# Experts' attention: the value product in quarters set between the two scores of a step, and four small products one step later

## What is computed

```python
def expert_step(acc, params):
    qw, qb_, kw, kb_, vw, vb_, ow, ob_, g = params
    q = (x @ qw.T + qb_).reshape(B, S, H, Dh).transpose(0, 2, 1, 3)
    ...
    scores = jnp.einsum('bhqd,bhkd->bhqk', q, k) * scale
    p = jax.nn.softmax(scores, axis=-1)
    o = jnp.einsum('bhqk,bhkd->bhqd', p, v)
    o = o.transpose(0, 2, 1, 3).reshape(B, S, E) @ ow.T + ob_
    return (acc + o * g[..., None], None)
```

## Time and profile before

| | |
|---|---|
| time, median of 3 runs | 2183.87 us (2181.33 to 2192.77) |
| profiled execution: its time, its span | 2187.13 us, 2185.3 us |
| mean granted TensorE clock | 0.942 |
| PE, DVE, ACT, POOL busy over the span | 85%, 77%, 59%, 43% |
| stage b, first and last record of the mix | 199.9 and 1098.8 us |

### The profile page before, as it was taken

The page is one execution under the profiler, slowest core; times in us unless marked ns, Lnnn a source line. Parts: engine busy times, 40 slices in busy tenths (PEclk is TensorE's granted clock), DMA queues, the critical chain, the costliest instruction groups (busy, mean ns, idle before and its releaser), DMA issues. The chain is left out here.

```text
span 2185.3 us, 50731 instructions
## 1 busy us (share of the span) xinstructions
PE 1855.6 (85%) x20464; PEld 954.8 (44%) x20464; DVE 1673.8 (77%) x2850; ACT 1288.2 (59%) x1848; POOL 941.1 (43%) x914
## 2 busy tenths in 40 slices
PE   5758999999999999999947898988888988988984
PEld 3542233233233333333223665665665655665663
DVE  3856777777777777777647978889878889879873
ACT  4423666666666666666725656666655656656652
POOL 0011111111111111111029958768768768768760
PEclk8956999999999999999968999999999999999998
DMA  1032223222323232323014333333333333333320
GB/s 36 1 76 50 49 57 58 50 55 55 64 60 65 60 64 60 64 60 61 2 39 119 89 95 103 100 96 107 95 96 103 100 95 103 100 96 102 95 69 15
DMA packets 101281, 156.36 MB, mean 72 GB/s; under 512 B 29335, under 2 KB 64185, under 8 KB 97209
## 3 DMA queue, kind: packets, MB, share of 16 engines
q1 hardware_dynamic: 98937, 152.19, 28.5%
q10 hardware_dynamic: 2112, 0.94, 0.3%
HBM read 98.03 MB, written 51.12 MB: 68 GB/s over the span
## 5 line engine op out<-in xcount | busy, mean ns | idle before, releaser
L824 DVE TENSOR_REDUCE ENM<-PM 128x1 f32<-128x512 f32 x1024 | 665.4, 687 | 212.3 <-PE PM L604 199.9
L735 ACT ACTIVATE EPT<-PA 128x1024 f32<-128x1024 f32 x512 | 514.6, 1021 | 214.7 <-PE PV L627 124.2
L604 PE MATMUL PM<-EKX,EQX 48*128 48x512 bf16 x1024 | 381.3, 393 | 18.9 <-DVE ENM L824 17.9
L1300 POOL TENSOR_TENSOR DRN<-DRN,DHALF 128x8 f32<-128x8 f32 x192 | 371.7, 1936 | 0.0
L524 POOL CAST ENMP<-ENM 128x16 bf16<-128x16 f32 x64 | 12.7, 198 | 748.0 <-DVE ENM L824 748.0
L627 PE MATMUL PV<-EPT,EVP 128*32 128x256 f32 x4096 | 327.9, 392 | 2.1 <-ACT EAVS L766 1.9
L1298 POOL TENSOR_TENSOR DQR<-DR 128x512 f32<-128x512 f32 x192 | 252.5, 1315 | 169.0 <-DVE DR L1581 169.0
L616 PE MATMUL PA<-EQX,EKX 51*128 51x512 bf16 x1024 | 254.6, 387 | 19.4 <-DMA EQX<-EROWS 15.4
L1344 PE MATMUL PM<-DWQKV,DXS 128*128 128x512 f32 x384 | 214.4, 641 | 26.9 <-ACT DRAW L1500 20.3
L604 PEld LDWEIGHTS PM<-EKX,EQX 48*128 48x128 bf16 x1024 | 93.8, 93 | 308.9 <-DVE ENM L824 222.0
L1500 ACT ACTIVATE DRAW<-PM 128x512 f32<-128x512 f32 x192 | 114.6, 597 | 169.5 <-DVE DR L1581 93.1
(11 more groups left out here) (207 smaller groups left out, 2858.2 us busy)
## 6 DMA issues: line engine op xcount, KB each, us to landing
DV<-d_vpark SPq DMA_DIRECT2D x192, 256.0 KB, 4.9
d_vpark<-DVT SPq DMA_DIRECT2D x48, 512.0 KB, 2.6
e_park<-EPARTS SPq DMA_DIRECT2D x64, 192.0 KB, 3.0
EQX<-e_park SPq DMA_DIRECT2D x32, 384.0 KB, 5.6
EKX<-e_park SPq DMA_DIRECT2D x32, 384.0 KB, 9.2
DWQKV<-in_WqkvR SPq DMA_DIRECT2D x6, 1536.0 KB, 10.0
e_park<-EPARTS SPq DMA_DIRECT2D x64, 128.0 KB, 2.7
e_park<-EPARTS SPq DMA_DIRECT2D x64, 64.0 KB, 2.1
```

Source lines behind the costliest of these rows:

```text
L604: pe.matmul(PM[:, r, :], lhsT=QX[64 * r:64 * r + KQ, b, hp, t * 128:(t + 1) * 128], rhs=KX[64 * r:64 * r + KQ, b, hp, :], start=True, stop ...
L735: s_.activation(PT[:, kt, pair * 2 * S:(pair + 1) * 2 * S], PA[:, 2 * pair:2 * pair + 2, :].rearrange("p a b -> p (a b)"), ACT.Exp, scale= ...
L824: v.tensor_reduce(NM[:, g % 2, t, j, 0:1], PM[:, r, :], AX.X, ALU.max, negate=True).then_inc(maxed, 1)
L1300: g.tensor_tensor(rn, rn, HALF[:, 0:8], ALU.pow).then_inc(rooted.sem, 1)
```

## The change

`mix` takes quarters of 128 queries in place of halves of 256; the count that its semaphore reaches doubles, and the waits of the exponential and of `mix_out` are rewritten to the same points. `key_major` takes the heads r that it is to do. In a step TensorE now does: `key_major` of head 0, a quarter, `key_major` of head 1, `query_major` r = 0, a quarter, `query_major` r = 1. In step 3 the two quarters stand behind everything, as the half did. The products for "v" and "ont" go from step 5 to 6 and "o" from 6 to 7, on TensorE, ACT and DVE.

```diff
     if g % HG == 1 and more:
-        u += [(5, "v")]
+        u += [(6, "v")]
     if g % HG == 0 and not (first and g == 0):
-        u += [(5, "ont"), (6, "o")]
+        u += [(6, "ont"), (7, "o")]
...
-                    for r in range(2):
+                    for r in rs:
                         mm = pe.matmul(PA[:, 2 * pair + r, :], lhsT=KX[64 * r:64 * r + KS, b, hp, kt * 128:(kt + 1) * 128],
                                        rhs=QX[64 * r:64 * r + KS, b, hp, :], start=True, stop=True)
-                    mm.then_inc(kscored, 1)
-
-                def mix(e, g, kt, half):
-
-                    k, c = e * NG + g, S // 2
+                    if 1 in rs:
+                        mm.then_inc(kscored, 1)
+
+                def mix(e, g, kt, part):
+                    k, c = e * NG + g, S // 4
...
                     for s in range(8):
-                        key_major(e, g, s)
+                        key_major(e, g, s, (0,))
+                        if s != 3:
+                            mixes(s, 0)
+                        key_major(e, g, s, (1,))
                         scores_ahead(s, (0,))
                         if s != 3:
-                            mixes(s)
+                            mixes(s, 1)
                         scores_ahead(s, (1,))
                         if s == 3:
-                            mixes(s)
+                            mixes(s, 0)
+                            mixes(s, 1)
...
-                        act.wait_ge(mixed, 8 * k + (2 * kt - 6))
+                        act.wait_ge(mixed, 16 * k + (4 * kt - 12))
...
-                    act.wait_ge(mixed, 8 * k + 8)
+                    act.wait_ge(mixed, 16 * k + 16)
...
-                        if s == 6 and "o" in uses:
+                        if s == 7 and "o" in uses:
                             add_out(gp // HG, use(e, g, "o"))
```

More of the change, by code:

```diff
@@ L605, in query_major, with key_major @@
                                   rhs=KX[64 * r:64 * r + KQ, b, hp, :], start=True, stop=True).then_inc(qscored, 1)
-                def key_major(e, g, s):
+                def key_major(e, g, s, rs):
                     f = (e * NG + g) * 8 + s
@@ L610, in key_major @@
                     hp = 2 * (g % HG) + pair
-                    if s == 0:
+                    if s == 0 and 0 in rs:
                         pe.wait_ge(rows_in, (e * NG + g) * 64 + 64)
-                    if not (isinstance(f, int) and f < 2):
+                    if 0 in rs and not (isinstance(f, int) and f < 2):
                         pe.wait_ge(exped, f - 1)
-                    for r in range(2):
+                    for r in rs:
                         mm = pe.matmul(PA[:, 2 * pair + r, :], lhsT=KX[64 * r:64 * r + KS, b, hp, kt * 128:(kt + 1) * 128],
                                        rhs=QX[64 * r:64 * r + KS, b, hp, :], start=True, stop=True)
-                    mm.then_inc(kscored, 1)
-                def mix(e, g, kt, half):
-                    k, c = e * NG + g, S // 2
+                    if 1 in rs:
+                        mm.then_inc(kscored, 1)
+                def mix(e, g, kt, part):
+                    k, c = e * NG + g, S // 4
                     pe.wait_ge(exped, k * 8 + (2 * kt + 2))
-                    if kt == 0 and half == 0 and not (isinstance(k, int) and k == 0):
+                    if kt == 0 and part == 0 and not (isinstance(k, int) and k == 0):
                         pe.wait_ge(mixed_out, k)
                     for j in range(4):
-                        mm = pe.matmul(PV[32 * j:32 * j + 32, half * c:half * c + c], lhsT=VP[:, g // HG, kt, 4 * (g % HG) + j, :],
-                                       rhs=PT[:, kt, j * S + half * c:j * S + half * c + c],
-                                       start=kt == 0 and half == 0, stop=kt == TB - 1, skip_group_check=True)
+                        mm = pe.matmul(PV[32 * j:32 * j + 32, part * c:part * c + c], lhsT=VP[:, g // HG, kt, 4 * (g % HG) + j, :],
+                                       rhs=PT[:, kt, j * S + part * c:j * S + part * c + c],
+                                       start=kt == 0 and part == 0, stop=kt == TB - 1, skip_group_check=True)
                     mm.then_inc(mixed, 1)
@@ L641, in scores_ahead, with mixes @@
                             query_major(e2, g2, s + LEAD - 16, rs)
-                    def mixes(s):
+                    def mixes(s, i):
                         kt, half = divmod(s - 3, 2)
                         if kt >= 0:
-                            mix(e, g, kt, half)
+                            mix(e, g, kt, 2 * half + i)
                         elif not (first and g == 0):
-                            mix(ep, gp, kt + TB, half)
+                            mix(ep, gp, kt + TB, 2 * half + i)
                     for s in range(8):
-                        key_major(e, g, s)
+                        key_major(e, g, s, (0,))
+                        if s != 3:
+                            mixes(s, 0)
+                        key_major(e, g, s, (1,))
                         scores_ahead(s, (0,))
                         if s != 3:
-                            mixes(s)
+                            mixes(s, 1)
                         scores_ahead(s, (1,))
                         if s == 3:
-                            mixes(s)
+                            mixes(s, 0)
+                            mixes(s, 1)
                         for step, what in slot_uses(first, last, g):
@@ L718, in _ @@
                     slot(NE - 1, g, False, True)
-                for kt, half in ((TB - 2, 1), (TB - 1, 0), (TB - 1, 1)):
-                    mix(NE - 1, NG - 1, kt, half)
+                for kt, part in ((TB - 2, 2), (TB - 2, 3)) + tuple((TB - 1, i) for i in range(4)):
+                    mix(NE - 1, NG - 1, kt, part)
                 pe.wait_ge(mixed_out, NE * NG)
```

## The result

The changed kernel takes 2296.2 us (median of 4, 2262.5 to 2338.1) against 2182.7 for the kernel before on the same chips; the ratio is 1.043 (95% interval 1.037 to 1.050). The forecast was 2206, in a range of 2186 to 2235: the direction was right, the size was not. The mean granted TensorE clock goes with the time: 0.883 (2338 us), 0.902 (2298), 0.903 (2295), 0.921 (2262), where the kernel before has 0.942.

A forecast was written before the change was run, and what follows sets the result against it. Stage b was taken as paced by TensorE in some steps, DVE or ACT in others, with TensorE pacing every step without another wait afterwards. Plain slots +20 and pairs +2 gave +22 us, 2206 on the median; range 2186 to 2235.

The forecast's parts named there:

- The price of a quarter: Stage b, TensorE: a quarter is 0.34 to 0.36 us long, taken as 0.36, with 0.32 on the way in.
- the step of 1.36: Stage b: a step at TensorE's own pace goes from 1.10 to 1.36 us, above DVE's 1.20.
- the late exponential: Plain slot: step 4's exponential on ACT starts at R + 1.63 instead of 1.13, delaying step 7 by 0.50 us.
- the sum of +22 at full clock: Whole kernel: +20 us from 32 plain slots and +2 us from 16 pairs of groups 0 and 1.
- the +0.64 of a plain slot: Groups 2, 3, 6, 7: from R (start of "rows") to the next R, 13.06 us instead of 12.42.
- The pair ends where it did, 0.07 later: Groups 0 and 1: where the wait for the rows' DMAs stands, the pair's end moves only 0.07 us.
- The waits for EON: Groups 0 and 1: moving "ont" and "v" takes away two waits of 0.98 us.
- DVE's wait for PM: Stage b: DVE's wait for scores in PM goes up from 185 us by some 20.
- Absorbed: Rival, plain slot: step 7 stays at 5.23, the slot costs +0.14, +6 us in all, 2190; chance 0.14.
- faster: Rival, stage b: a quarter with way in costs 0.445, half of a half; 18 us faster, 2166; chance 0.12.
- the loads bind: Rival, stage b: a quarter takes the half's 0.57, step 1.78, about 2390 us; chance 0.04.
- dearer meetings: Rival, stage b: each new meeting of kinds costs 0.05 to 0.1 more, 2235 to 2265 us; chance 0.08.

The follow-up runs named there:

- the pair of filled kernels: Unread products ahead of the rows' wait in group 2, added to the changed kernel (2238.7 us) and to the kernel before (2213.6 us).
- quarters_between_keys: Changed kernel with both quarters of a step together between the two `key_major`: 2239.4 us, ratio 1.026.
- quarters_dense_behind: Changed kernel with five unread 128 x 512 float32 products behind step 0 of group 2: 2270.7 us, ratio 1.043.

## Why the prediction was wrong

- **The step that failed** is one sentence of the sum: "Clock: stage b is at 1.00 and the gaps shrink, so no change." I read 1.00 as a property of a busy engine, and so put the clock into the sum at nothing. It was one of the old order, which had the full clock back 3.4 us after each of its two falls. The new order does not: in the profiled execution 300 us of stage b ran at 1.2 GHz, where a step is 2.26 instead of 1.36 us. By 1 - 1.36 / 2.26 = 0.40 of 300 that is about 120 of the 147 us by which stage b grew; 25 are the dearer order, as the pair of filled kernels shows. That is the longest of the four runs; the median grew by 114 us, with less low clock.
- The gaps did not vanish either: the rows' wait stood at 0.8 to 2.4 us in group 2 of all later experts (4.5 in the first). A wait of 1.57 us was enough once, and was not another time.
- The price of a quarter, the step of 1.36, the late exponential and the sum of +22 at full clock held: 0.36, 1.36, R + 1.63 and 25.1 us. But the +0.64 of a plain slot (0.68 measured) came right with a wrong share in it. I had put 0.50 on the late exponential and taken the dearer steps 4 to 6 as hidden behind it. Measured, these steps alone bring step 7 to R + 5.50, and the exponential adds 0.12.
- Groups 0 and 1: 17.11 for group 0, and 14.39 for a group 5, which has the jobs of group 1 and mostly no wait; forecast 17.14 and 14.26. "The pair ends where it did, 0.07 later" does not hold: in the second to the seventh expert, all at full clock there, groups 0 and 1 took 0.4 to 1.6 us longer with their wait. Groups 4 and 5 took 0.8 less to 0.1 more where they ran at full clock, so little of this shows in the sum. That the wait hangs on SP's loads was an assumption too: swapping them gained no time. What ends that wait stays open.
- The waits for EON are gone, as forecast. DVE's wait for PM went to 319 us, not to 205: that is the low clock again.
- Of the rivals none had the clock in it. "Absorbed", "faster", "the loads bind" and "dearer meetings" were answered by the 0.36 of a quarter, the 0.32 on the way to it and the step of 1.36; that the measured time comes near the 2235 to 2265 of the last says nothing for it. The rule of the Trainium skill that a change of tiling mode drains TensorE ("TensorEngine Tiling (Array Packing)", Key Properties) agrees with the trace at full clock so far as each change from scores to mix costs 0.10 over the streaming; that it is a drain, no run shows.

What stays open: which property of the alternated order keeps the clock down, the number of changes of kind as such or the time that is lost in each. With two changes a step and the same quarters it came back within 10 us, with three on average it took up to 38 us, and with four 20 to 147 us, but for one stretch of 3.4 us; the two go together in all kernels. Also open: why a wait of 1.57 us was followed by a fall in one expert and not in another, why projections ended some stretches and not the longest at its first pair, and what made the clock fall without a long wait in quarters_between_keys.

## What to carry to other kernels

The granted clock is a state with a history. Before an edit that keeps TensorE busy but cuts its work finer, ask two things of the trace: where does it wait for a microsecond or more, and how fast does the clock come back there now. A change that costs 1% at full clock cost 4 to 5% here, and the busy share rose. To price such a change, fill the wait with work in both kernels and compare those two: here it took the clock of this stage, and most of the spread, out of the difference. Compare them only with each other; both were slower behind the stage than the kernel before, by 16 and 19 us, for a reason not known.

## What the runs showed of the hardware

- TensorE stayed at 1.2 GHz for 147 us while it was busy for 145 of them. Being busy did not bring the clock back. It came back at products of 128 x 512 in float32 over the full array, at all four returns of the changed kernel and in all five of quarters_dense_behind. But one pair of such products passed at 1.2 GHz and 93 more us at 1.2 GHz followed, and in other kernels five stretches of 20 to 38 us ended without them.
- Waits of 1.4 to 1.6 us between the starts of matmuls were followed by a fall in some places and not in others of the same kernel. In quarters_between_keys the clock fell with no such wait, TensorE busy for 7.39 of the 8.60 us before.
- Eight records of 128 columns in four column tiles take 0.13 us from the first four to the second and 0.22 from there to the next score; each change from scores to mix costs 0.10 us over the 0.21 of streaming.
- DMA issues on ACT's queue started 0.01 us after the start of the exponential ahead of them where ACT had been idle, and 0.12 after it where it had not, which moved everything behind them by 0.11.
